# Two factorizations in one: the Gram matrix on the lower 64 partitions, the top block two steps behind on the upper 64

## The chip, the core and the metric

The kernel runs on one core of a Trainium2 chip. The core has TensorE (PE, matrix products), VectorE (DVE), ScalarE (ACT), GpSimd (POOL) and SyncE (SP, whose queue issues most of the transfers). The metric is the time of one execution in device microseconds (us). Less is better.

## The reference

An AdaLN transformer block over 16 batch items of 128 tokens with 144 channels, and then a rotation of its result in a subspace:

```python
x = _L0_cond_ref(x, cond[:, None, :], ...)   # layer norm, 16-head attention, MLP; shifts, scales, gates from cond
U, _ = jnp.linalg.qr(P)                      # P is 144 x 64
R = _rotation(cond, W, b)                    # expm of a skew 64 x 64 matrix, one for each item
z = jnp.einsum('btn,nd->btd', x, U)
z_rot = jnp.einsum('btd,bde->bte', z, R)
x_rot = x + jnp.einsum('btd,nd->btn', z_rot - z, U)
```

The change touches only `qr(P)`. The kernel takes U from an elimination of the Gram matrix G = P^T P (64 x 64). The signs that a Householder QR would give U's columns come from a second elimination, of the top 64 x 64 block B of P. B's elimination needs, at each step, the pivot of G's same step (its square root and the sign of B's own pivot give a shift of B's diagonal).

## The kernel before, in words

All instructions stand in an order written by hand, one stream for each engine, and semaphores connect them. An engine works through its stream in order: whatever stands behind a waiting instruction waits with it. After a front part (loads, modulations, weights transposed) comes a loop over b = 0 to 17, in which attention of item b, the rest of item b-1 and the output side of item b-2 are interleaved in four quarters q = 0 to 3. After it comes the MLP with the rotation. In the quarters of the loop stand also, one by one, the 64 steps of the elimination (`STEPS`: steps 0 to 2 stand in the front part, steps 3 to 63 in the quarters, with q = 3 left out at b = 4, 9 and 14), and from b = 0 on the stages of the matrix exponential.

The tile Z holds, on all 128 partitions, three blocks of 64 columns: G, an identity that becomes the inverse factor, and B. The matrices stand twice, on partitions 0 to 63 and again on 64 to 127. One step of the elimination does this:

- TensorE (`step_rows`) brings row k of G and row k-1 of B to all partitions: two products with a column of the identity repeated 128 times (lines 1440 and 1444), each an fp32 product that the trace shows as two MATMUL records.
- VectorE (`eliminations`) runs nine operations: G's step k and B's step k-1, interleaved, since B's step needs G's pivot of the step before. `s_Gstep` and `s_Bstep` tell that Z is updated.
- GpSimd computes in `square_root` the power -1/2 of the reciprocal pivot (line 412) and its double negated (413), and in `masked_column` B's column below the diagonal (417).

TensorE waits for the steps in `rows_read`, before each pair of step products. VectorE's quarters hold besides the step the maxima of the scores (`maximum`, line 969), layer norms and other work; the softmax maxima are what TensorE waits for next. The SyncE queue first issues the loads, then the store of the gates to memory and the load that spreads them over 128 partitions (`gates`, lines 331 and 334), then the 63 rows of the generator (`A<-v`, line 341), which VectorE reads in quarter 3 of b = 4 (`triangles`), and then waits for the outputs.

## Time and profile before

| | |
|---|---|
| median of 3 runs | 321.51 us (319.87 to 322.42) |
| span of the profiled execution | 323.8 us |
| TensorE busy | 282.6 us |
| VectorE busy | 212.7 us |
| ScalarE busy | 130.7 us |
| GpSimd busy | 105.0 us |
| mean granted clock of TensorE | 0.935 of full |

The span runs from the first to the last instruction of the profiled execution, which took 2.3 us more than the median run. A busy time is the time in which at least one of the engine's instructions ran. PEld is the loading of the stationary operand, which runs beside the products. The chain is the way back from the last instruction, at each step to what released it.

### The profile page before, as it was taken

How to read it: one execution, taken by the hardware profiler on the slowest of the kernel's cores; microseconds unless marked ns; L12 is line 12 of the kernel's file. 1: busy time of each engine (PE TensorE's matmuls, PEld its weight loads, DVE VectorE, ACT ScalarE, POOL GpSimd, SP SyncE). 2: the span in 40 equal slices, each digit the busy share in tenths (PEclk: the TensorE clock that was granted, in tenths of full speed). 3: DMA queues.
4: the chain of work that ended last, by engine and by line, in shares of the span. 5: the costliest groups of instructions: out<-in, count | busy, mean ns of one | idle time of the engine just before them, and what ended most of it. 6: DMA issues, size and time to landing. Idle time of an engine off the chain costs nothing.

```text
span 323.8 us, 8835 instructions
## 1 busy us (share of the span) xinstructions
PE 282.6 (87%) x3215; PEld 204.5 (63%) x3215; DVE 212.7 (66%) x948; ACT 130.7 (40%) x274; POOL 105.0 (32%) x298
## 2 busy tenths in 40 slices
PE   2898889879899998888998889989987489999995
PEld 2765355566666766647777567677775344756983
DVE  6147654785777998748997697757575665733543
ACT  1023323442555445416554444555444316340321
POOL 7413141524233324224442234323234088500000
PEclk9998967985999999959999999999999769999999
DMA  7936000000000000000000000000000000000013
GB/s 200 241 98 257 3 10 0 11 9 10 1 3 2 2 3 2 2 0 4 3 2 2 3 2 2 1 4 3 2 2 1 2 0 2 4 0 0 2 38 109
DMA packets 9779, 8.44 MB, mean 26 GB/s; under 512 B 2064, under 2 KB 9334, under 8 KB 9608
## 3 DMA queue, kind: packets, MB, share of 16 engines
q1 hardware_dynamic: 9380, 7.11, 7.7%
q10 hardware_dynamic: 356, 0.75, 0.8%
q8 instruction: 27, 0.44, 0.6%
q14 instruction: 16, 0.13, 0.1%
HBM read 6.40 MB, written 1.20 MB: 23 GB/s over the span
## 4 chain that ended last, share of the span: by engine, by line
PE 70%; DVE 20%; issue 6%; ACT 2%; POOL 1%; ACTq 1%; DVEq 0%
PE banks L1330 6%; PE banks L1440 6%; PE banks L1366 5%; PE banks L1598 5%; PE banks L1335 5%; PE banks L1331 5%; PE banks L1582 4%; PE banks L1198 4%; PE banks L1378 4%; PE banks L1444 3%; PE banks L1394 3%; DVE qstk L969 2%; DVE cB L914 2%; PE banks L1415 2%; PE banks L1404 2%
## 5 line engine op out<-in xcount | busy, mean ns | idle before, releaser
L412 POOL TENSOR_TENSOR root<-rec,mhalf 128x1 f32<-128x1 f32 x63 | 34.5, 548 | 151.0 <-DVE Z L910 151.0
L969 DVE TENSOR_REDUCE qstk<-banks 128x8 f32<-128x1024 f32 x32 | 39.0, 1219 | 7.9 <-PE banks L1366 6.3
L895 DVE RECIPROCAL rec<-banks 128x1 f32<-128x1 f32 x63 | 10.3, 164 | 46.0 <-PE banks L1444 43.0
L551 ACT ACTIVATE E<-banks 128x1024 f32<-128x1024 f32 x32 | 32.8, 1026 | 9.0 <-PE banks L1378 8.8
L1440 PE MATMUL banks<-Z,ident 128*128 128x65 f32 x126 | 26.6, 295 | 9.2 <-DVE Z L916 8.7
L1440 PEld LDWEIGHTS banks<-Z,ident 128*128 128x128 f32 x126 | 20.3, 201 | 18.5 <-issue 12.0
L1378 PEld LDWEIGHTS banks<-QM,KT 32*128 32x128 f32 x512 | 18.0, 193 | 16.5 <-issue 16.4
L1378 PE MATMUL banks<-QM,KT 32*128 32x128 f32 x512 | 24.2, 305 | 2.4 <-issue 2.4
L1366 PE MATMUL banks<-KT,QT 32*128 32x128 f32 x512 | 24.8, 310 | 1.7 <-DVE wskT L714 1.6
L1444 PE MATMUL banks<-Z,ident 128*128 128x64 f32 (+62 forms) x126 | 24.0, 272 | 0.4 <-DVE Z L916 0.4
L1366 PEld LDWEIGHTS banks<-KT,QT 32*128 32x128 f32 x512 | 18.4, 197 | 8.3 <-issue 8.3
L1394 PE MATMUL banks<-E,V 128*32 128x128 f32 x512 | 21.9, 292 | 1.4 <-ACT E L551 0.7
L1444 PEld LDWEIGHTS banks<-Z,ident 128*128 128x128 f32 x126 | 20.3, 202 | 0.6 <-issue 0.6
L1335 PE MATMUL banks<-ident,qstk 128*128 128x128 f32 x128 | 20.1, 282 | 0.0
L1330 PE MATMUL banks<-wqkv,hT 128*128 128x432 f32 x32 | 19.9, 709 | 0.0
L1598 PE MATMUL banks<-wfc2a,gT 128*128 128x144 f32 x128 | 18.6, 288 | 0.0
L1598 PEld LDWEIGHTS banks<-wfc2a,gT 128*128 128x128 f32 x128 | 16.7, 190 | 2.3 <-issue 2.3
L543 ACT ACTIVATE qstk<-banks 128x144 f32<-128x144 f32 x16 | 4.9, 309 | 32.2 <-PE banks L1331 32.2
L910 DVE SCALAR_TENSOR_TENSOR Z<-banks,cG,Z 128x64 f32<-128x64 f32 x63 | 17.8, 282 | 0.0
L509 ACT ACTIVATE hT<-banks,mod 128x128 f32<-128x128 f32 (+1 forms) x32 | 12.5, 445 | 12.9 <-PE banks L1317 12.9
L1331 PE MATMUL banks<-wqkv,hT 128*128 128x432 f32 x32 | 17.5, 633 | 0.0
L916 DVE SCALAR_TENSOR_TENSOR Z<-banks,cB,Z 128x63 f32<-128x63 f32 (+62 forms) x63 | 15.8, 251 | 2.2
(249 smaller groups left out, 627.2 us busy)
## 6 DMA issues: line engine op xcount, KB each, us to landing
gates<-gates_dram SPq DMA_DIRECT2D x1, 2304.0 KB, 9.7
x_all<-in_x_dram SPq DMA_DIRECT2D x4, 288.0 KB, 6.1
out_dram<-x_all SPq DMA_DIRECT2D x8, 144.0 KB, 2.0
wskew<-in_L_cond_W_dram SPq DMA_DIRECT2D x4, 283.5 KB
A<-v SPq DMA_DIRECT2D x63, 4.0 KB
wada<-in_L_cond_W_ada_dram ACTq DMA_DIRECT2D x1, 432.0 KB
wfc1a<-in_L_cond_W_fc_dram SPq DMA_DIRECT2D x1, 288.0 KB
wfc2a<-in_L_cond_W_fc_dram SPq DMA_DIRECT2D x1, 288.0 KB
```

The costliest lines, as they stand in the source:

```text
L412: link(nc.gpsimd.tensor_tensor(root[:, at], rec[:, at], mhalf[:, 0:1], ALU.pow))
L551: nc.scalar.activation(E[:, g, :, :, :].rearrange("p r j t -> p r (j t)"), scored(g), ACT.Exp).then_inc(s_E, 1)
L969: nc.vector.tensor_reduce(qstk[b % 2][:, 8 * g:8 * g + 8, D:D + 1].rearrange("p (j r) a -> p r (j a)", r=4), scored(g).rearrange("p r (j m ...
L1330: mm(bank[4][:, 0:3 * C], hT1[:, :], wqkv1[:, :], start=True, stop=False)
L1331: mm(bank[4][:, 0:3 * C], hT2[:, :], wqkv2[:, :], start=False, stop=True).then_inc(s_qkv, 1)
L1335: ins = pe.transpose(dst[:, 128 * j:128 * j + 128], stack[:, 4 * j:4 * j + 4, :].rearrange("p h s -> p (h s)"), ident[:, :])
L1366: ins = mm(bank[r][:, 128 * j:128 * j + 128], QT[rows, 2 * g + j, :], KT[b % 3][rows, 2 * g + j, :], start=True, stop=True)
L1378: ins = mm(bank[r][:, 128 * j:128 * j + 128], KT[b % 3][rows, 2 * g + j, :], QM[rows, 2 * g + j, :], start=True, stop=True)
L1394: ins = mm(bank[6][own, cols], weights[:, first:first + 32], E[:, g, 2 * (i % 2) + p, i // 2, :], start=(p == 0), stop=(p == 1))
L1440: mm(bank[7][:, cols], ident[:, k:k + 1].to_broadcast([128, 128]), Z[:, cols], start=True, stop=True).then_inc(s_Grow, 1)
L1444: mm(bank[7][:, cols], ident[:, k - 1:k].to_broadcast([128, 128]), Z[:, cols], start=True, stop=True).then_inc(s_Brow, 1)
L1598: mm(dst, gT[Q % 2][:, k, cols], wfc2a[:, k, :], start=(k == 0), stop=False)
```

## The change

G stays on partitions 0 to 63 and B moves to partitions 64 to 127, in the same columns but shifted by `SKEW` = 2: B's step k-2 is done in the same instructions as G's step k. So Z has 130 columns in place of 192, the steps are 65 in place of 64 (`LAST` = 64), and each has one chain of five VectorE operations over both halves. They are written in one form: a pivot is shifted by a signed amount, and for G that amount is zero, for B it is what G's step of two before gave. These four numbers for each of 64 rows travel in a DMA of 1 KB from `sent` (partitions 0 to 63) to `got` (partitions 64 to 127), with four buffers (`SHIFTS`). GpSimd now runs `elimination(k)`: the power, then `column_taken(k + 1)` (which waits for the transfer of step k-1), and two small operations that fill `sent`. The SyncE queue issues the 63 transfers, and the generator's 63 rows stand between them, seven at a time behind those of steps 11 to 19. The row products are 64x64 tiles. The skipped quarters are gone, and the last step stands at b = 15, q = 1. P and the Gram product are no longer doubled. At the end the two diagonals, now on different halves, are reduced into two columns and brought to all partitions by two small products.

The core of the diff:

```diff
     VS, VO = 48, 16
     SQ = 4
+    SKEW, SHIFTS = 2, 4
...
-        cB, c, w = sb("cB", [128, 1]), sb("c", [128, 1]), sb("w", [128, 1])
-        dG, dB, usc = sb("dG", [128, RD]), sb("dB", [128, RD]), sb("usc", [128, 4])
...
 
         v = sb("v", [B, NSK + 1])
         A0, Bm = sb("A0", [128, NC, RD]), sb("Bm", [128, NC, RD])
...
+                if FIRST + len(STEPS) <= LAST:
                     STEPS[b, q] = FIRST + len(STEPS)
-        assert FIRST + len(STEPS) == RD and max(STEPS) <= (B, 0)
+        assert FIRST + len(STEPS) == LAST + 1 and max(STEPS) <= (B, 0)
+
+        lower, upper_half, everywhere = slice(0, 64), slice(64, 128), slice(0, 128)
+
+        def half_of(k):
+
+            return lower if k < SKEW else everywhere if k < RD - 1 else upper_half
 
         def columns_left(k):
 
-            return slice(k + 1, RD + k + 1), slice(2 * RD + k, 3 * RD)
+            return slice(k + 1, RD + k + 1 if k < RD - 1 else RD + SKEW)
 
...
-            for i in range(RD - 1):
+            def generator_row(i):
                 at = (RD - 1) * i - i * (i - 1) // 2 - i
                 sp.wait_ge(s_v, min(4, (at + RD - 2) // 504 + 1))
                 sp.dma_start(A0[i:i + RD + 1:RD, :, :], v[:, at:at + RD]).then_inc(s_win, 16)
+
+            sp.wait_ge(k_fill, 8)
+            for j in range(RD - 1):
+                sp.wait_ge(s_sent, j + 1)
+                sp.dma_start(got[upper_half, j % SHIFTS, :], sent[:, j % SHIFTS, :]).then_inc(s_got, 16)
+                if ROWS_FROM <= j < ROWS_FROM + 9:
+                    for i in range(7 * (j - ROWS_FROM), 7 * (j - ROWS_FROM) + 7):
+                        generator_row(i)
 
...
+            def elimination(k):
+
+                own, at = sent[:, k % SHIFTS, :], slice(k, k + 1)
+                if k < RD - 1:
+                    pool.wait_ge(s_coef, k + 1)
+                    wait(pool, s_got, 16 * (k - SHIFTS + 1))
+                    rooted = lk.mark(nc.gpsimd.tensor_tensor(own[:, 2:3], rec[lower, at], mhalf[lower, 0:1], ALU.pow))
+                if k < LAST:
+                    pool.wait_ge(s_step, k + 1)
+                    column_taken(k + 1)
+                if k < RD - 1:
+                    lk.need(rooted)
+                    link(nc.gpsimd.tensor_tensor(own[:, 3:4], own[:, 2:3], coef[lower, at], ALU.mult))
+                    nc.gpsimd.tensor_tensor(own[:, 0:2], own[:, 2:4], own[:, 2:4], ALU.add).then_inc(s_sent, 1)
 
...
             def eliminations(k):
-                G, B = k < RD - 1, k > 0
-
-                if B:
-                    j, jp = bass.ds(k - 1, 1), bass.ds(k - 1 + 2 * RD, 1)
-                    bkk = bank[7][:, jp]
-                    dve.wait_ge(s_Brow, k)
-                if G:
-                    kk = bass.ds(k, 1)
-                    dve.wait_ge(s_Grow, k + 1)
-                    got_rec = lk.mark(nc.vector.reciprocal(rec[:, kk], bank[7][:, kk]))
-                if B:
-                    wait(dve, s_zm, k)
-                    got_c = lk.mark(STT(c[:, :], bkk, cG[:, j], zm[:, :], ALU.mult, ALU.subtract))
-                    wait(dve, s_root, k)
-                    got_sign = lk.mark(TS(cB[:, :], bkk, 0.0, nroot2[:, j], ALU.is_ge, ALU.mult))
-                if G:
-                    lk.need(got_rec)
-                    got_cG = lk.mark(TS(cG[:, kk], Z[:, kk], rec[:, kk], negmask[:, kk], ALU.mult, ALU.mult))
-                if B:
-                    lk.need(got_sign)
-                    got_pivot = lk.mark(STT(w[:, :], cB[:, :], root[:, j], bkk, ALU.add, ALU.subtract))
-                if G:
-                    lk.need(got_cG)
-                    cols = columns_left(k)[0]
-                    STT(Z[:, cols], bank[7][:, cols], cG[:, kk], Z[:, cols], ALU.mult, ALU.add).then_inc(s_Gstep, 1)
-                if B:
-                    lk.need(got_pivot)
-                    link(nc.vector.reciprocal(w[:, :], w[:, :]))
-                    link(STT(cB[:, :], c[:, :], w[:, :], cG[:, j], ALU.mult, ALU.add))
-                    cols = columns_left(k)[1]
-                    STT(Z[:, cols], bank[7][:, cols], cB[:, :], Z[:, cols], ALU.mult, ALU.add).then_inc(s_Bstep, 1)
+                own, at, cols = half_of(k), slice(k, k + 1), columns_left(k)
+                pivot = bank[7][own, at]
+                dve.wait_ge(s_row, k + 1)
+                dve.wait_ge(s_col, k + 1)
+                shift = got[own, (k - SKEW) % SHIFTS, :]
+                link(STT(signed[own, :], pivot.to_broadcast([own.stop - own.start, 2]), 0.0, shift[:, 0:2], ALU.is_ge, ALU.mult))
+                link(STT(den[own, :], pivot, signed[own, 0:1], shift[:, 2:3], ALU.add, ALU.subtract))
+                link(nc.vector.reciprocal(rec[own, at], den[own, :]))
+                TS(coef[own, at], signed[own, 1:2], rest[own, :], rec[own, at], ALU.add, ALU.mult).then_inc(s_coef, 1)
+                dve.wait_ge(s_coef, k + 1)
+                STT(Z[own, cols], bank[7][own, cols], coef[own, at], Z[own, cols], ALU.mult, ALU.add).then_inc(s_step, 1)
 
...
-                pe.wait_ge(s_ldP, 64)
-                mm(bank[7][:, 0:RD], twice(p1[:, :, :]), p1[:, 0, :], start=True, stop=False)
-                mm(bank[7][:, 0:RD], twice(p2[:, :, :]), p2[:, 0, :], start=False, stop=True)
-                mm(bank[7][:, RD:2 * RD], twice(p1[0:RD, :, :]), ident[0:RD, 0:RD], start=True, stop=True)
-                mm(bank[7][0:RD, 2 * RD:2 * RD + C1], p1[:, 0, :], ident[:, :], start=True, stop=True)
-                mm(bank[7][0:RD, 2 * RD + C1:2 * RD + C], p2[:, 0, :], ident[0:C2, 0:C2], start=True, stop=True).then_inc(s_Gp, 1)
+                pe.wait_ge(s_ldP, 32)
+                mm(bank[7][lower, 0:RD], p1[:, :], p1[:, :], start=True, stop=False)
+                mm(bank[7][lower, 0:RD], p2[:, :], p2[:, :], start=False, stop=True)
+                mm(bank[7][upper_half, 0:RD], p1[0:RD, :], ident[0:RD, 0:RD], start=True, stop=True)
+                mm(bank[7][0:RD, 2 * RD:2 * RD + C1], p1[:, :], ident[:, :], start=True, stop=True)
+                mm(bank[7][0:RD, 2 * RD + C1:2 * RD + C], p2[:, :], ident[0:C2, 0:C2], start=True, stop=True).then_inc(s_Gp, 1)
 
             pe.wait_ge(s_sil, 2)
             pe.transpose(bank[6][0:C1, 0:B], sil[:, 0:C1], ident[0:B, 0:B])
...
             def step_rows(k):
 
                 rows_read(k)
-                if k < RD - 1:
-                    cols = slice(k, RD + k + 1)
-                    mm(bank[7][:, cols], ident[:, k:k + 1].to_broadcast([128, 128]), Z[:, cols],
-                       start=True, stop=True).then_inc(s_Grow, 1)
-                if k > 0:
-                    cols = slice(2 * RD + k - 1, 3 * RD)
-                    mm(bank[7][:, cols], ident[:, k - 1:k].to_broadcast([128, 128]), Z[:, cols],
-                       start=True, stop=True).then_inc(s_Brow, 1)
+                own, cols = half_of(k), slice(k, columns_left(k).stop)
+                if own != upper_half:
+                    ins = mm(bank[7][lower, cols], ident[lower, k:k + 1].to_broadcast([RD, RD]), Z[lower, cols], start=True, stop=True)
+                if own != lower:
+                    at = RD + k - SKEW
+                    ins = mm(bank[7][upper_half, cols], ident[upper_half, at:at + 1].to_broadcast([RD, RD]), Z[upper_half, cols],
+                             start=True, stop=True)
+                ins.then_inc(s_row, 1)
 
...
             def U_parts(b, part):
                 if part == 0:
-                    pe.wait_ge(s_Bstep, RD - 1)
+                    pe.wait_ge(s_step, LAST + 1)
                     pe.wait_ge(s_QT, B)
                     pe.transpose(bank[4][0:RD, 512 - RD:512], Z[0:RD, RD:2 * RD], ident[0:RD, 0:RD]).then_inc(s_ETp, 1)
+                    pe.wait_ge(s_dred, 2)
+                    for own in (lower, upper_half):
+                        ins = mm(bank[4][own, 512 - RD - 2:512 - RD], eye2[:, :], dcol[:, :], start=True, stop=True)
+                    ins.then_inc(s_dgp, 1)
                 if part == 1:
                     pe.wait_ge(s_ET, 2)
+                    pe.wait_ge(s_dg, 1)
                     mm(bank[4][:, 0:C], twice(ET[:, :, :]), PT[:, :], start=True, stop=True).then_inc(s_UTp, 1)
                 if part == 2:
                     pe.wait_ge(s_UT, 2)
```

On TensorE, quarters 1 and 2 of block b = 5. A row names out and in by their tiles (Osb, kstk, qstk, KT, QT, E and V belong to the attention, A to the generator) and gives partitions and columns of the moving operand. Lines 1440 and 1444 are the step's row products. Before:

```order
L1404 MATMUL banks<-ident,Osb 128x128 x2
L1440 MATMUL banks<-Z,ident 128x65
L1444 MATMUL banks<-Z,ident 128x42
L1335 MATMUL banks<-ident,kstk 128x128 x4
L1335 MATMUL banks<-ident,qstk 128x128 x4
L1366 MATMUL banks<-KT,QT 128x128 x8
L1394 MATMUL banks<-E,V 32x128 x8
L1204 MATMUL banks<-eye,A 64x64 x16
L1440 MATMUL banks<-Z,ident 128x65
L1444 MATMUL banks<-Z,ident 128x41
```

After, the same place:

```order
L1412 MATMUL banks<-ident,Osb 128x128 x2
L1447 MATMUL banks<-Z,ident 64x65
L1450 MATMUL banks<-Z,ident 64x65
L1343 MATMUL banks<-ident,kstk 128x128 x4
L1343 MATMUL banks<-ident,qstk 128x128 x4
L1374 MATMUL banks<-KT,QT 128x128 x8
L1402 MATMUL banks<-E,V 32x128 x8
L1212 MATMUL banks<-eye,A 64x64 x16
L1447 MATMUL banks<-Z,ident 64x65
L1450 MATMUL banks<-Z,ident 64x65
```

The pair of step products keeps its place. Each of the two is now a 64-partition tile with 65 columns at every step, where the second of the pair had 42 and 41 columns here.

On VectorE, the first step of block b = 0 and what stands around it: `wskT` is the last copy of the front part, `qstk` the first maximum. Before:

```order
L714 COPY wskT<-banks 16x504
L969 TENSOR_REDUCE qstk<-banks 128x4x2
L895 RECIPROCAL rec<-banks 128x1
L898 SCALAR_TENSOR_TENSOR c<-banks,cG,zm 128x1
L900 TENSOR_SCALAR cB<-banks,nroot 128x1
L903 TENSOR_SCALAR cG<-Z,rec,negmask 128x1
L906 SCALAR_TENSOR_TENSOR w<-cB,root,banks 128x1
L910 SCALAR_TENSOR_TENSOR Z<-banks,cG,Z 128x64
L913 RECIPROCAL w<-w 128x1
L914 SCALAR_TENSOR_TENSOR cB<-c,w,cG 128x1
L916 SCALAR_TENSOR_TENSOR Z<-banks,cB,Z 128x61
```

After:

```order
L739 COPY wskT<-banks 16x504
L977 TENSOR_REDUCE qstk<-banks 128x4x2
L916 SCALAR_TENSOR_TENSOR signed<-banks,got 128x2
L917 SCALAR_TENSOR_TENSOR den<-banks,signed,got 128x1
L918 RECIPROCAL rec<-den 128x1
L919 TENSOR_SCALAR coef<-signed,rest,rec 128x1
L921 SCALAR_TENSOR_TENSOR Z<-banks,coef,Z 128x64
```

The step's nine rows are five, and each waits for the one before it; the place of the step behind the maximum is the same.

On the SyncE queue, from the store of the gates on. Before:

```order
L331 DMA gates_dram<-gates_sb 16x288
L334 DMA gates<-gates_dram 128x4608
L341 DMA A<-v 2x8x64 x63
L346 DMA out_dram<-x_all 128x2x144 x8
L93 UNCONDITIONAL_BRANCH
```

After (the pattern of seven generator rows and one `got` goes on nine times, and the rest of the `got` rows follow):

```order
L336 DMA gates_dram<-gates_sb 16x288
L339 DMA gates<-gates_dram 128x4608
L350 DMA got<-sent 64x4 x12
L345 DMA A<-v 2x8x64 x7
L350 DMA got<-sent 64x4
L345 DMA A<-v 2x8x64 x7
L350 DMA got<-sent 64x4
L345 DMA A<-v 2x8x64 x7
```

The transfers of the steps stand behind the load of the gates, and the generator's rows stand between them.

## Rows read from the trace of the kernel before

**Rows 1.** The page: busy times, TensorE clock, and the chain that ended last.

```profile
PE 282.6 (87%) x3215; PEld 204.5 (63%) x3215; DVE 212.7 (66%) x948; ACT 130.7 (40%) x274; POOL 105.0 (32%) x298
...
PEclk9998967985999999959999999999999769999999
...
PE 70%; DVE 20%; issue 6%; ACT 2%; POOL 1%; ACTq 1%; DVEq 0%
PE banks L1330 6%; PE banks L1440 6%; PE banks L1366 5%; PE banks L1598 5%; PE banks L1335 5%; PE banks L1331 5%; PE banks L1582 4%; PE banks L1198 4%; PE banks L1378 4%; PE banks L1444 3%; PE banks L1394 3%; DVE qstk L969 2%; DVE cB L914 2%; PE banks L1415 2%; PE banks L1404 2%
```

**Rows 2.** The chain in order of time, 110 to 170 us: start us, us, what.

```profile
116.69 0.17 PE banks L1440 x2
116.86 0.21 PE banks L1444 x2
...
120.87 0.17 DVE rec L895
...
121.88 0.23 DVE cB L914
...
122.14 0.27 DVE Z L916
122.40 0.14 issue
122.54 0.41 PE banks L1440 x2
122.94 0.20 PE banks L1444 x2
...
132.12 1.08 PE banks L1198 x32
133.20 0.37 PE banks L1440 x2
```

**Rows 3.** The page, costliest groups: line engine out<-in count | busy, mean ns | idle before.

```profile
L412 POOL TENSOR_TENSOR root<-rec,mhalf 128x1 f32<-128x1 f32 x63 | 34.5, 548 | 151.0 <-DVE Z L910 151.0
```

**Rows 4.** DMA issues: what, queue, count, KB each, median us to landing.

```profile
gates<-gates_dram SPq DMA_DIRECT2D x1, 2304.0 KB, 9.7
x_all<-in_x_dram SPq DMA_DIRECT2D x4, 288.0 KB, 6.1
...
p<-in_L_cond_P_dram SPq DMA_DIRECT2D x2, 4.0 KB, 4.3
...
gates_dram<-gates_sb SPq DMA_DIRECT2D x1, 18.0 KB, 1.4
cond_sb<-in_cond_dram SPq DMA_DIRECT2D x1, 9.0 KB, 2.1
```

**Rows 5.** Timeline, VectorE, 26 to 28.5 us: end of step 2, last weight copy.

```profile
27.34 0.28 DVE L916 SCALAR_TENSOR_TENSOR Z<-banks,cB,Z 128x62 f32<-128x62 f32 x1
27.54 0.66 DVE L714 COPY wskT<-banks 16x504 f32<-16x504 f32 x1
```

**Rows 6.** Timeline, TensorE: the first scores.

```profile
28.34 0.73 PE L1366 MATMUL banks<-KT,QT 32*128 32x128 f32 x16 [1.57 <-DVE wskT L714]
```

**Rows 7.** Timeline, SyncE queue: the load of the gates, the first generator rows.

```profile
22.91 0.34 SPq L334 DMA_DIRECT2D gates<-gates_dram  x1
37.60 4.45 SPq L341 DMA_DIRECT2D A<-v  x8
```

**Rows 8.** Windows of 2 us: busy times and counts, PEclk, DMA share, GB/s.

```profile
26.00:28.00 2.00, 0.77 (x8) 0.45 (x5) 1.93 (x11) 1.19 (x3) 0.87 (x3) 1.00 0.87 304
...
30.00:32.00 2.00, 2.00 (x4) 0.76 (x4) 1.74 (x10) 0.00 (x0) 0.67 (x2) 0.50 0.15 65
```

**Rows 9.** Timeline, VectorE: the first instruction of step 11.

```profile
62.82 0.16 DVE L895 RECIPROCAL rec<-banks 128x1 f32<-128x1 f32 x1
```

**Rows 10.** Timeline, TensorE: the row product in quarter 0 of block 5.

```profile
100.52 0.43 PE L1440 MATMUL banks<-Z,ident 128*128 128x65 f32 x2
```

**Rows 11.** Timeline, VectorE, quarter 0 of block 16: the inverse factor copied.

```profile
246.48 0.35 DVE L948 COPY ET<-banks 64x64 f32<-64x64 f32 x2 [1.70 <-PE banks L1469]
```

More of the change, by code:

```diff
@@ L382, in _ @@
                 diagonal(eye2[own, :], own)
-            for own in (lo, hi):
-                below_diagonal(negmask[own, :], own, -1.0)
+            for own, base in ((lo, 0), (hi, -SKEW)):
+                below_diagonal(below[own, :], own, -1.0, base)
             for own in (lo, hi):
@@ L456, in attention @@
                         scales_of_U()
+            pool.wait_ge(s_Z, 4)
+            column_taken(0)
             for k in range(FIRST):
-                square_root(k)
-                masked_column(k)
+                elimination(k)
             for b in range(0, B + 2):
```

90 lines of the change are left out of this document (44 added, 46 removed).

## The prediction

> **What bounds the kernel now.** I began with the page. TensorE is busy for 87% of the span, and the chain that ended last is 70% TensorE and 20% VectorE [rows 1]. So the reader should see a kernel in which one in-order engine sets most of the time and another holds it up at places. The elimination is in both shares. Its row products (L1440 and L1444) are 6% and 3% of the chain, some 29 us, and one operation of the VectorE step (L914) alone is 2%, some 6.5 us, which at 0.23 us each [rows 2] is 28 steps. Counted piece by piece, the chain goes through 51 pairs of row products and about 25 VectorE steps. Split by time (28 to 61, 61 to 100, 100 to 246 us) they are 7, 9 and 35 pairs, and 4, 6 and 15 steps. What the change does to these is its gain. GpSimd and the SyncE queue are nearly absent from the chain, and the change puts both into the loop of the steps. That is where its cost must be looked for.
>
> **Row products.** On the chain a pair costs 0.38 us where the work ahead has the same tile shape (0.17 + 0.21) and 0.61 us when it follows a wait (0.41 + 0.20); the mean over the 35 late pairs is 0.52 [rows 2]. The new pair is four records of 64x64 tiles. Such tiles stand in the trace: 32 of L1198 take 1.08 us, 0.034 each, and the 128x128 product behind them takes 0.37 in place of 0.17, so a change of tile shape costs 0.2 us [rows 2]. The new pair is then 0.14 us, plus some 0.06 on the way in and 0.15 to 0.2 on the way out: 0.34 on the mean, a gain of 0.18. Between the score products and the values it gains more; in quarter 1, which had no change of shape before, it gains nothing. Bounds: if the two halves don't overlap, 0.47 (gain 0.05); if the way out is hidden, 0.2 (gain 0.3).
>
> **VectorE step.** From the first operation to the end of Z the nine operations take 122.41 - 120.87 = 1.54 us, two chains interleaved. The five new ones wait for one another. A dependent operation costs 0.26 us from start to start (121.88 to 122.14) [rows 2], a reciprocal less, so I take four times 0.24 plus 0.27: 1.23 us, a gain of 0.3. Bounds: five ninths of 1.54 (gain 0.7) and no gain.
>
> **GpSimd's column.** VectorE's next step now waits also for `column_taken`, which stands behind the power (0.55 us [rows 3]) on GpSimd. The power starts with `coef`, some 0.3 us before Z is done, so the column is ready about 0.55 us after Z. TensorE's way from the end of Z to the next step is 0.14 + 0.61 us before [rows 2] and about 0.5 after. The two are level, and I charge nothing; if GpSimd is 0.2 us later, the waited steps cost 0.2 x 25 = 5 us.
>
> **The transfer.** It is issued after the column of step k+1 is taken, and the column of step k+2 waits for it. So a column can follow the last after 0.65 us on GpSimd plus the transfer L. The smallest transfers in the trace took 1.4 us (18 KB, the queue empty) and 2.1 us (9 KB read from memory) [rows 4]; I take L = 1.8, nearer to neither. The loop is then 2.45 us (2.05 to 2.75). The steps of quarters 1 and 3 in a late block stand 122.54 - 116.69 = 5.85 us apart, 2.9 us for one [rows 2], and after the change 2.8 with the gains above. So in these blocks the transfer costs nothing at L = 1.8, and nothing up to L = 2.15. The Trainium skill (DMA: Bandwidth & Descriptors, section "Anatomy of one DMA — SWDGE (gpsimd) path") gives a fixed cost of about 2.0 us for one DMA. With that as L the loop would be 2.65 us, still under 2.8, and only the landing in the paragraph on the generator's rows would move, by 0.2 us, which makes the forecast 322.2; no transfer of this size stands in the trace of before to decide it.
>
> **The start.** The first transfer is needed by step 2, which stands on VectorE ahead of the last weight copy, and TensorE's first scores wait for that copy [rows 5, 6]. On SyncE it stands behind the load of the gates, issued at 22.9 us [rows 7] and landed 9.7 us later [rows 4], at 32.6. That a small transfer waits for a large one on its queue shows in P's 4 KB, which took 4.3 us behind the 288 KB of x_all, against 1.4 on an empty queue [rows 4]. I let the transfer land at 32.0 (31.0 to 32.9: most of the gates' bytes have moved by 31 [rows 8]). Then come column 0.3, step 1.2, copy 0.66 and the semaphore 0.14: scores at 34.3 in place of 28.34, **+6.0 us** (0 if it isn't held).
>
> **The generator's rows.** Eight take SyncE 4.45 us, 0.55 each [rows 7]. Seven and one transfer (0.45) are 4.3 us, and this goes on nine times, while the twelve quarters from step 11 to block 5 take 100.5 - 62.8 = 37.7 us, 3.1 each [rows 9, 10]. Step 11 starts at 62.8, so its transfer goes out at 65.1 (step 1.54, GpSimd 0.75), and that of step 20 at 65.1 + 9 x 4.3 = 103.8. It lands at 105.6; step 22 starts at 105.9 and ends at 107.1; TensorE's next row product, in quarter 0 of block 5, starts at 107.3 in place of 100.52, **+6.8 us**. The queue is behind from the second transfer on, so what the steps gain between 61 and 100 us (9 x 0.18 + 6 x 0.3 = 3.4) is lost in it and not counted. Bounds: +6 to +8, by L.
>
> **Small terms.** Three of the Gram products load half the columns: -0.7 us, hidden by nothing. Steps now stand in the quarters 3 of blocks 9 and 14 (+1.0) and none in quarters 2 and 3 of block 15, where the chain went through the last two steps (-1.6). At the end TensorE and VectorE wait for the diagonals (two products, a copy; a like pair of copies is 0.35 [rows 11]): +1.0.
>
> **The clock.** TensorE idled from 26.8 to 28.3 us [rows 6], and soon after, the granted clock was 0.5 of full, 1.2 GHz in place of 2.4 [rows 8]. The page's clock line has several such dips [rows 1]. The 7 us of idling at the start and the waits in blocks 3 and 4 should lengthen them: +1.5 us (0 to 7).
>
> **The sum.** Gains outside blocks 2 to 4: pairs 42 x 0.18 = 7.6, steps 19 x 0.3 = 5.7: -13.3. Against them +6.0 + 6.8 + 1.0 + 1.5, and -0.7 - 0.6: 323.8 + 0.7 = 324.5 us of span. The profiled execution was 2.3 us above the median, so the forecast is **322 us**: what the steps gain is spent on the SyncE queue.
>
> **Rivals.**
> - Not held: the first transfer passes the gates' load, since its 64 short pieces share the engines with it. The 4.3 us of P speak against that. It gives 322.2 - 6.0 = 316 us.
> - Bigger gain: VectorE's step near 1.0 us and the way out hidden. 42 x 0.1 + 19 x 0.2 = 8 more, 314 us. For it speaks that 28 steps lie on the chain; against it the four dependencies.
> - **Transfer-bound (slower):** on the GpSimd-SyncE loop, with L = 2.4 us the loop takes 3.05 us, 0.25 more than a late step would have. Over the 42 steps behind the generator's rows that is +10.5 us: 332 us. It decides from L = 2.15 on. The 2.1 us of a small load [rows 4] are close to that; the 1.4 us of the store speak against it.
> - Clock: the new idling keeps TensorE at 1.2 GHz through half of blocks 3 to 5. The dips on the page's clock line to 5 and 6 in ten [rows 1] show that it can stay down for whole slices of 8 us. +5: 327 us.
> - The halves don't overlap, so that the pair does not do what it is made for: 42 x 0.13 = +5.5, 328 us.
>
> **How the numbers follow.** A measurement of this kernel can tell about 1%, 3.2 us, from no change. Forecast 0.37 (318.5 to 324.7); not held 0.14; bigger gain 0.13; transfer-bound 0.12; clock 0.18; no overlap 0.06. Faster by over 1%: 0.27. Within: 0.37. Slower: 0.36. With cases of both signs the forecast's own range stands beside the full one: 313 takes in both faster cases; 330 takes in the clock and the overlap case and leaves out most of the transfer-bound one and the tails of the others, under 2 in 10.
>
> **What would show it.** The first `got` should land after 31 us, with TensorE idle from 27 to 34. In blocks 2 to 4 the `got` issues should be 4.3 us apart, and GpSimd's column should be what VectorE waits for. Later blocks should be 0.8 to 1 us shorter than the 12.2 of before, with `column_taken` waiting for no transfer; the four records of a pair should start within 0.15 us. I am wrong if the start has no hole, if the generator rows are issued faster between transfers, or if late steps wait for `got`.

## The result and the profile after

The changed kernel takes **334.1 us** (median of 4 runs, 331.0 to 335.6) against 320.7 us (318.9 to 322.4) for the kernel before: a ratio of 1.040, 95% interval 1.032 to 1.049. It is slower, and above the forecast's range. Some executions of each kernel run up to 3% longer at a lower granted clock; the ranges here hold all runs, the ratios leave those out. The experiments were run later, in four groups, each beside the kernel before. Its medians there are 323 to 325 us with a wider spread (319 to 330), but its fastest run is 319.0 to 320.1 in every group, and 318.9 above. The changed kernel was not run again, so an experiment's distance from its 334.1 is a distance between groups.

The page of the changed kernel, in the parts that answer to [rows 1, 3, 4] (on top its span, then busy times, clock, chain, costliest groups, DMA issues):

```profile
span 332.7 us, 8806 instructions
...
PE 270.1 (81%) x3219; PEld 184.6 (55%) x3219; DVE 192.9 (58%) x709; ACT 130.5 (39%) x274; POOL 125.8 (38%) x363
...
PEclk9998599999779589799999997999979769999999
...
PE 40%; issue 14%; DMA 12%; SPq 11%; POOL 11%; DVE 9%; ACT 1%; ACTq 1%; POOLq 0%; DVEq 0%
DMA got<-sent 11%; SPq L345 9%; PE banks L1610 5%; POOL rest L425 4%; PE banks L1594 4%; PE banks L1374 3%; PE banks L1206 2%; PE banks L1338 2%; POOL sent L434 2%; PE banks L1386 2%; PE banks L1339 2%; PE banks L1343 2%; PE banks L1402 2%; PE banks L1447 1%; POOL sent L441 1%
...
L916 DVE SCALAR_TENSOR_TENSOR signed<-banks,got 128x2 f32<-128x2 f32 (+1 forms) x65 | 10.1, 156 | 67.8 <-POOL rest L425 41.1
L425 POOL TENSOR_SCALAR rest<-Z,below,got 128x1 f32<-128x1 f32 (+1 forms) x65 | 26.0, 400 | 49.2 <-DMA got<-sent 47.4
...
L1374 PE MATMUL banks<-KT,QT 32*128 32x128 f32 x512 | 25.5, 317 | 9.2 <-DVE wskT L739 9.1
L1447 PE MATMUL banks<-Z,ident 64*64 64x65 f32 x126 | 20.6, 245 | 13.3 <-DVE Z L921 12.8
...
gates<-gates_dram SPq DMA_DIRECT2D x1, 2304.0 KB, 9.8
...
got<-sent SPq DMA_DIRECT2D x63, 1.0 KB, 1.6
A<-v SPq DMA_DIRECT2D x63, 4.0 KB
```

Read it from the chain. TensorE's share falls from 70% to 40%, and VectorE's from 20% to 9%. In their place stand the transfer (`got`, 11%), the SyncE queue's row issues (L345, 9%) and GpSimd (11%). The work itself did become cheaper (TensorE is busy for 12.5 us less, VectorE for 20), but the chain left it. The groups name the waits in their order: GpSimd's column waited 47.4 us for transfers, VectorE's step 41.1 us for the column, TensorE 12.8 us for the step. Between 62 and 126 us the chain is nearly half (49.3%) row issues of line 345.

The start, in the timelines of the SyncE queue, GpSimd, VectorE and TensorE (start us, us, what, idle before and its releaser):

```profile
23.09 0.34 SPq L339 DMA_DIRECT2D gates<-gates_dram  x1
23.54 11.02 SPq L350 DMA_DIRECT2D got<-sent  x2
...
33.26 0.39 POOL L425 TENSOR_SCALAR rest<-Z,below,got 128x1 f32<-128x1 f32 x1 [8.08 <-DMA got<-sent]
...
33.76 0.16 DVE L916 SCALAR_TENSOR_TENSOR signed<-banks,got 128x2 f32<-128x2 f32 x1 [7.68 <-POOL rest L425]
...
34.72 0.28 DVE L921 SCALAR_TENSOR_TENSOR Z<-banks,coef,Z 128x64 f32<-128x64 f32 x1
34.92 0.66 DVE L739 COPY wskT<-banks 16x504 f32<-16x504 f32 x1
...
35.72 1.24 PE L1374 MATMUL banks<-KT,QT 32*128 32x128 f32 x16 [9.08 <-DVE wskT L739]
```

The first transfer, 1 KB, is issued 0.45 us behind the load of the gates and lands 9.6 us later. TensorE's first scores are at 35.72 in place of 28.34 [rows 6], and take 1.24 us in place of 0.73, since TensorE was granted 1.2 GHz (0.50) from 36 to 38 us.

The generator's rows, in the timelines of the SyncE queue, VectorE and TensorE, from 90 us:

```profile
90.06 0.53 SPq L350 DMA_DIRECT2D got<-sent  x1
90.63 3.76 SPq L345 DMA_DIRECT2D A<-v  x7
94.44 0.53 SPq L350 DMA_DIRECT2D got<-sent  x1
...
107.53 0.53 SPq L350 DMA_DIRECT2D got<-sent  x1
...
93.44 0.16 DVE L916 SCALAR_TENSOR_TENSOR signed<-banks,got 128x2 f32<-128x2 f32 x1 [4.36 <-POOL rest L425]
...
94.73 0.27 PE L1447 MATMUL banks<-Z,ident 64*64 64x65 f32 x1 [3.44 <-DVE Z L921]
```

From 90 us on a transfer leaves every 4.37 us, and one step of the elimination follows each. Windows of the changed kernel by stage, from the first scores of block 0, 3, 4, 5, 6 and 15 to the next (columns as in [rows 8]), and under them those of the kernel before for the same stages:

```profile
35.72:74.40 38.68, 33.04 (x335) 18.55 (x335) 24.59 (x93) 15.36 (x33) 16.85 (x52) 0.94 0.02 3
74.40:90.56 16.16, 11.46 (x139) 7.55 (x138) 8.46 (x33) 5.98 (x14) 6.42 (x19) 0.89 0.04 8
90.56:108.47 17.91, 11.60 (x140) 7.51 (x139) 7.81 (x27) 6.00 (x14) 5.48 (x18) 0.90 0.05 9
108.47:126.08 17.61, 14.03 (x172) 9.31 (x171) 9.75 (x34) 5.99 (x14) 6.18 (x21) 0.71 0.02 2
126.08:240.62 114.54, 103.01 (x1632) 74.39 (x1631) 81.15 (x275) 59.06 (x126) 53.86 (x166) 0.97 0.02 3
240.62:332.70 92.08, 77.90 (x702) 54.05 (x701) 47.24 (x161) 30.89 (x62) 23.86 (x50) 0.93 0.05 14
```

```profile
28.34:75.12 46.78, 41.20 (x335) 26.65 (x335) 31.04 (x153) 15.71 (x33) 13.61 (x43) 0.80 0.06 22
75.12:89.33 14.21, 12.93 (x139) 9.29 (x139) 8.59 (x42) 5.79 (x14) 4.39 (x14) 0.81 0.02 5
89.33:99.87 10.54, 10.02 (x136) 7.30 (x135) 8.60 (x38) 6.09 (x14) 4.14 (x15) 1.00 0.01 3
99.87:112.14 12.27, 11.51 (x171) 8.81 (x170) 9.50 (x43) 5.91 (x14) 3.53 (x12) 1.00 0.01 1
112.14:232.71 120.57, 109.53 (x1623) 83.41 (x1623) 91.41 (x404) 59.26 (x127) 42.13 (x128) 0.97 0.01 2
232.71:323.80 91.09, 77.80 (x707) 54.35 (x707) 49.66 (x180) 30.75 (x62) 24.72 (x54) 0.94 0.05 14
```

The 8.9 us between the two spans are +7.4 at the start, -8.1 in blocks 0 to 2, +14.7 in blocks 3 to 5, -6.0 in blocks 6 to 14, and +1.0 behind. Much of the -8.1 is the clock (0.80 there before, 0.94 after). Experiment 10 is the kernel before with its late steps left out, the same up to block 8. Its blocks 0 to 2 take 41.1 us and its blocks 3 to 5 35.2 (here 46.8 and 37.0). Against that trace the change is -2.4 and +16.5. Of the -6.0, 4.1 us lie in block 8 (15.3 before, 11.2 after), where the granted clock was 0.79 before and 1.00 after.

The medians lie 4.5 us further apart than the spans. In the runs that have both, the time is some 1.8 us more than the span. The profiled execution before, by its span of 323.8, was then one of some 325.6 us, 4.9 above its median, by those low clocks; the one after took 334.5, 0.4 above. (The 2.3 us that were counted between the profiled and the median run set a span against a time. Time against time they are 4.1, and the forecast stays what it is, since its own span of 324.5 is a time of 326.3.)

### The profile page after: what moved, and what is told of

The parts are those of the page before. It is cut to its first block, busy times and chain, and to the rows that moved or that the text cites. A ratio compares the mean times of both kernels' runs of the same rounds, so it can differ in the third digit from the quotient of the medians.

```text
span 332.7 us, 8806 instructions
## 1 busy us (share of the span) xinstructions
PE 270.1 (81%) x3219; PEld 184.6 (55%) x3219; DVE 192.9 (58%) x709; ACT 130.5 (39%) x274; POOL 125.8 (38%) x363
## 4 chain that ended last, share of the span: by engine, by line
PE 40%; issue 14%; DMA 12%; SPq 11%; POOL 11%; DVE 9%; ACT 1%; ACTq 1%; POOLq 0%; DVEq 0%
DMA got<-sent 11%; SPq L345 9%; PE banks L1610 5%; POOL rest L425 4%; PE banks L1594 4%; PE banks L1374 3%; PE banks L1206 2%; PE banks L1338 2%; POOL sent L434 2%; PE banks L1386 2%; PE banks L1339 2%; PE banks L1343 2%; PE banks L1402 2%; PE banks L1447 1%; POOL sent L441 1%
## 5 line engine op out<-in xcount | busy, mean ns | idle before, releaser
L434 POOL TENSOR_TENSOR sent<-rec,mhalf 64x1 f32<-64x1 f32 x63 | 34.6, 550 | 85.4 <-DVE coef L919 85.4
L916 DVE SCALAR_TENSOR_TENSOR signed<-banks,got 128x2 f32<-128x2 f32 (+1 forms) x65 | 10.1, 156 | 67.8 <-POOL rest L425 41.1
L425 POOL TENSOR_SCALAR rest<-Z,below,got 128x1 f32<-128x1 f32 (+1 forms) x65 | 26.0, 400 | 49.2 <-DMA got<-sent 47.4
L1447 PE MATMUL banks<-Z,ident 64*64 64x65 f32 x126 | 20.6, 245 | 13.3 <-DVE Z L921 12.8
L1447 PEld LDWEIGHTS banks<-Z,ident 64*64 64x64 f32 x126 | 12.4, 137 | 26.0 <-issue 13.3
L1450 PE MATMUL banks<-Z,ident 64*64 64x65 f32 (+2 forms) x126 | 20.6, 244 | 0.0
L921 DVE SCALAR_TENSOR_TENSOR Z<-banks,coef,Z 128x64 f32<-128x64 f32 (+2 forms) x65 | 18.3, 282 | 2.3
L1338 PE MATMUL banks<-wqkv,hT 128*128 128x432 f32 x32 | 19.1, 685 | 0.0
L919 DVE TENSOR_SCALAR coef<-signed,rest,rec 128x1 f32<-128x1 f32 (+1 forms) x65 | 17.7, 273 | 2.4
L1343 PEld LDWEIGHTS banks<-ident,qstk 128*128 128x128 f32 x128 | 15.4, 145 | 6.4 <-issue 6.2
L533 ACT ACTIVATE hT<-banks,mod 128x128 f32<-128x128 f32 (+1 forms) x32 | 12.5, 444 | 11.9 <-PE banks L1325 11.9
```

Source lines behind the costliest of these rows:

```text
L425: nc.gpsimd.tensor_scalar(rest[own, :], Z[own, at], below[own, at], got[own, (k - SKEW) % SHIFTS, 3:4], ALU.mult, ALU.subtract).then_inc(s ...
L434: rooted = lk.mark(nc.gpsimd.tensor_tensor(own[:, 2:3], rec[lower, at], mhalf[lower, 0:1], ALU.pow))
L1338: mm(bank[4][:, 0:3 * C], hT1[:, :], wqkv1[:, :], start=True, stop=False)
L1343: ins = pe.transpose(dst[:, 128 * j:128 * j + 128], stack[:, 4 * j:4 * j + 4, :].rearrange("p h s -> p (h s)"), ident[:, :])
L1447: ins = mm(bank[7][lower, cols], ident[lower, k:k + 1].to_broadcast([RD, RD]), Z[lower, cols], start=True, stop=True)
```

## The experiments

Theory A is the forecast's own: what is late is the SyncE queue, where the transfers stand behind the gates' load and then behind seven rows each. Rivals: the DMA engines are full whatever the queue (B), the clock and the operations queued behind GpSimd's waiting column (C, L), and the transfer's latency in every step (D). The edits are of the changed kernel unless said. The starts of each block's first scores, in us, are read from one execution each; those of 3, 4 and 11 are the longest of their runs (324.4, 323.0 and 309.8 us):

| kernel | median | b0 | b3 | b5 | b6 | b9 | b15 | span |
|---|---|---|---|---|---|---|---|---|
| before | 320.7 | 28.3 | 75.1 | 99.9 | 112.1 | 154.4 | 232.7 | 323.8 |
| changed | 334.1 | 35.7 | 74.4 | 108.5 | 126.1 | 163.2 | 240.6 | 332.7 |
| 1 gates, ScalarE's queue | 330.8 | 28.2 | 71.7 | 105.6 | 121.6 | 157.3 | 234.6 | 326.4 |
| 2 gates, pieces | 323.4 | 27.8 | 66.2 | 100.7 | 113.9 | 149.6 | 227.0 | 320.6 |
| 3 rows spread | 321.2 | 35.9 | 74.8 | 99.0 | 116.2 | 153.3 | 230.4 | 322.6 |
| 4 skew four | 319.0 | 27.9 | 66.0 | 91.4 | 112.5 | 149.6 | 226.3 | 321.2 |
| 5 = 2 + 3 | 313.6 | 28.2 | 66.8 | 92.2 | 104.2 | 139.9 | 217.6 | 311.2 |
| 6 = 2 + 3 + 4 | 311.5 | 30.3 | 66.3 | 87.4 | 104.6 | 140.3 | 215.6 | 309.9 |
| 7 zeroing first | 331.5 | 34.1 | 74.3 | 108.7 | 123.8 | 159.3 | 237.1 | 330.6 |
| 11 = 6 + later masking | 306.5 | 30.0 | 66.6 | 88.6 | 100.1 | 137.2 | 214.0 | 308.0 |
| 12 = 5 + later masking | 310.6 | 27.7 | 67.3 | 92.1 | 104.2 | 139.9 | 215.8 | 308.0 |

### 1. The gates' load on ScalarE's queue

```diff
-            sp.dma_start(gates[:, :, :].rearrange("p b n -> p (b n)"),
-                         gd.to_broadcast([128, B * 2 * C])).then_inc(s_gld, 16)
...
                 generator_weights(n)
+                if n == 0:
+                    act.wait_ge(s_gst, 16)
...
+                    act.dma_start(gates[:, :, :].rearrange("p b n -> p (b n)"),
+                                  gd.to_broadcast([128, B * 2 * C])).then_inc(s_gld, 16)
```

> Only edit: the 2304 KB load of gates is issued by ScalarE's queue (behind its first copy of the generator's weights) instead of SyncE's, so that the small transfers of got no longer stand behind it in a queue. Theory A (the order of one queue made the start late): the first transfer lands about 2 us after its issue at 23.5, the first scores start near 28.5 to 29.5 instead of 35.7, and the run is 5 to 7 us below the changed kernel's 334.1: 327 to 329. Rival B (the load fills the 16 DMA engines, whichever queue it is in): the first transfer still takes 7 us or more, first scores after 33, 331 to 334.

Measured: 330.8 us (328.2 to 335.6). ScalarE's queue, GpSimd and TensorE in its timelines:

```profile
23.38 0.35 ACTq L622 DMA_DIRECT2D gates<-gates_dram  x1
...
33.54 0.37 POOL L421 TENSOR_SCALAR rest<-Z,below,got 128x1 f32<-128x1 f32 x1 [5.71 <-DMA got<-sent]
...
28.24 0.73 PE L1375 MATMUL banks<-KT,QT 32*128 32x128 f32 x16 [1.31 <-DVE wskT L740]
...
35.32 0.37 PE L1448 MATMUL banks<-Z,ident 64*64 64x65 f32 x1 [4.45 <-DVE Z L922]
```

The transfer issued ahead of the load passes (1.65 us), and the scores are at 28.24. The next one, issued at 26.3 us, takes 7.1 us with no load ahead of it on its queue, and the hole comes back one step later: block 0 takes 17.9 us in place of 13.3. So A named the wrong thing. B was right in that the wait is for the load itself, and another queue only moves it; its late first scores (after 33) did not come, since here the first transfer goes out ahead of the load. The Trainium skill (DMA: Bandwidth & Descriptors, section "Queues, rings and completion order") says that each DMA engine serves the queues in turns, a whole packet of descriptors at a time. If an engine's share of this load were one packet or little more, that would account for the 7.1 us; no run here shows the packets' bounds.

### 2. The gates' load in sixteen pieces

```diff
-            sp.dma_start(gates[:, :, :].rearrange("p b n -> p (b n)"),
-                         gd.to_broadcast([128, B * 2 * C])).then_inc(s_gld, 16)
+
+            def gates_piece(b):
+                sp.dma_start(gates[:, b, :], gates_dram[b:b + 1, :].to_broadcast([128, 2 * C])).then_inc(s_gld, 16)
...
                 sp.dma_start(got[upper_half, j % SHIFTS, :], sent[:, j % SHIFTS, :]).then_inc(s_got, 16)
+                if j < B // 2:
+                    gates_piece(2 * j)
+                    gates_piece(2 * j + 1)
```

> Only edit: the load of gates is cut into 16 loads of 144 KB, two behind each of the first eight transfers of got on SyncE's queue. Each transfer then stands behind at most two loads (about 1.2 us together, a 16th of 9.8 us each). Theory A (one queue's order) and rival B (the DMA engines are full) both expect the first scores near 29 to 31 and 327 to 330 for the run; if it stays above 332, the start isn't what costs and the gain of an earlier start is given back in blocks 3 to 6.

Measured: 323.4 us (322.2 to 325.9), 10.7 below the changed kernel, and below the 327 to 330 that both theories expected. No transfer takes over 2.8 us up to 60 us, and the scores are at 27.8. Block 0 takes 11.4 us at the full 2.4 GHz (13.3 at 0.83 in the changed kernel). This belongs to the hole: wherever the start is late by it (the changed kernel, 3, 7, 8) block 0 takes 13.2 to 13.4 us at 0.79 to 0.83, and wherever the load is in pieces (2, 5, 6, 11, 12) 11.3 to 11.4 at 1.00. So the hole costs 7.9 + 1.9 us, more than its own length. The trace has 4.0 us less in blocks 3 to 5 too, all in block 5 (13.2 for 17.6), and 1.5 more in blocks 1 and 2. Those 4.0 us can't be put down to the hole, since experiment 8 has the hole and a block 5 of 12.5 us (rows in the next section).

### 3. The generator's rows, four behind each of 16 transfers

```diff
-        ROWS_FROM = FIRST + 8
+        ROWS_FROM = FIRST + 3
-                if ROWS_FROM <= j < ROWS_FROM + 9:
-                    for i in range(7 * (j - ROWS_FROM), 7 * (j - ROWS_FROM) + 7):
+                if ROWS_FROM <= j < ROWS_FROM + 16:
+                    for i in range(4 * (j - ROWS_FROM), min(4 * (j - ROWS_FROM) + 4, RD - 1)):
```

> Only edit: the 63 generator rows are issued 4 behind each of 16 transfers (steps 6 to 21) instead of 7 behind each of 9 (steps 11 to 19). SyncE's cycle in that stretch is then 0.5 + 4 x 0.54 = 2.7 us instead of 4.37. Theory A (SyncE's issues set the pace of blocks 2 to 5): the steps no longer come 4.37 us apart, block 6 starts 8 to 13 us earlier than the changed kernel's 126.1 relative to block 2, and the run gives 321 to 326. Rival C (the stage is late through the throttled clock and through what is queued behind the waiting column on GpSimd, whatever the rows' number): 330 to 334.

Measured: 321.2 us (319.6 to 324.4), 13.0 below. Blocks 3 and 4 take 12.5 and 11.7 us in place of 16.2 and 17.9. Theory A holds, and C does not: neither the start's hole nor the operations behind the column were touched. Nor is the length of these blocks a matter of the clock. In the five traces with seven rows behind each of nine transfers at a skew of two (the changed kernel, 1, 2, 7, 8) blocks 3 and 4 together take 33.9 to 34.6 us, at granted clocks from 0.69 to 0.90. Blocks 3, 4 and 5 of experiment 8, which is the changed kernel up to block 8:

```profile
76.63:91.75 15.12, 12.04 (x140) 8.13 (x139) 7.64 (x29) 5.99 (x14) 6.09 (x17) 0.77 0.04 7
91.75:110.83 19.08, 14.15 (x139) 9.61 (x138) 7.91 (x27) 5.98 (x14) 5.78 (x19) 0.73 0.05 8
110.83:123.36 12.53, 10.91 (x171) 7.66 (x171) 9.76 (x34) 5.99 (x14) 5.93 (x21) 1.00 0.02 3
```

In experiment 3 block 5 stays long (17.1 us, 0.80 of the clock); VectorE waits 2.3 us for the last rows there, of which experiments 6 and 11 show more.

### 4. A skew of four steps

```diff
-    SKEW, SHIFTS = 2, 4
+    SKEW, SHIFTS = 4, 8
```

with one semaphore for each of four transfers in flight, and without GpSimd's wait for an old transfer ahead of the power.

> Only edit: the upper half runs four steps behind instead of two (eight slots for the carried values, one semaphore for each of four transfers in flight, two steps more at the end), so that a column waits for a transfer three steps old. Gates load and generator rows stay as they are. Theory D (in the late blocks the transfer's latency in the loop GpSimd, SyncE, DMA, GpSimd eats the gain): blocks 7 to 15 shorten by 0.5 to 0.8 us each, 5 to 8 us, and the start gains 2 to 5 us as steps 1 to 3 wait for no transfer; in all 320 to 328. Rival E (late blocks are bound by other work, the wait for the transfer has cover): blocks 7 to 15 shorten by less than 0.2 us each, and only the start gains: 329 to 333.

Measured: 319.0 us (316.4 to 323.0), 15.1 below, below what either theory expected. The gates' load still holds the first transfer for 9.6 us, but no step up to 3 needs it, and the hole is gone. Blocks 8 to 14 keep their lengths (11.2, 11.5, 14.5, 12.7, 13.3, 12.5, 12.2 us against 11.2, 11.6, 14.6, 12.7, 13.3, 12.5, 12.7). The sum that E made, 329 to 333, was wrong by blocks 3 and 4, which a deeper skew also shortens (25.4 us for 34.1); block 5 is longer (21.0 for 17.6), with a wait of 5.1 us for the last rows. But D falls and E holds for what they were to tell apart: in the late blocks the transfer's latency is covered at a skew of two, though GpSimd waits for it there (14.8 us in 21 waits behind 126 us, in the changed kernel).

### 5 and 6. Both repairs, at a skew of two and of four

> Both repairs of SyncE's queue together, at the change's own skew of two steps: gates in 16 pieces behind the first eight transfers, and the generator rows 4 behind each of 16 transfers. The loads of gates end with step 7, the rows begin at step 6, so in two steps both stand behind a transfer. Each repair alone gave 323.4 and 321.2 against the changed kernel's 334.1. Theory F (the two delays are separate, 7.5 us at the start and 9 to 13 us in blocks 3 to 5, and the rest is the granted clock): together 310 to 316. Rival G (what one saves, the other loses: TensorE's clock or the steps' chain takes a part back, as the load on ScalarE's queue did, where the start gained 7.5 and block 0 lost 4.6): 317 to 322.

> Both repairs and a skew of four steps (the sum of the three edits). If a transfer is still waited for in blocks 0 to 5 at a skew of two, with 4 rows behind each, this lies 2 to 4 us under the kernel with both repairs at skew two; if the two steps' slack already covers it, the two are the same within 1 us. In blocks 8 to 15 the length of a block should not change, as it didn't with the skew alone (11.2, 11.5, 14.5, 12.7, 13.3, 12.5, 12.2 against 11.2, 11.6, 14.6, 12.7, 13.3, 12.5, 12.7).

Measured: 313.6 us (313.0 to 314.3) at a skew of two, 0.979 of the kernel before (0.971 to 0.987); 311.5 at four (three runs of 311.2 to 312.1 and one of 305.8), at the near edge of the 2 to 4 us that it was to gain if the transfers were still waited for. Theory F holds: the two delays nearly add up (10.7 + 13.0 = 23.7 apart, 20.6 together). At a skew of four block 5 takes 17.2 us. VectorE and TensorE in that trace:

```profile
91.41 0.69 DVE L752 TENSOR_TENSOR A<-A,upper 128x512 f32<-128x512 f32 x1 [3.55 <-DMA A<-v]
...
93.34 1.23 PE L1390 MATMUL banks<-QM,KT 32*128 32x128 f32 x16 [2.75 <-issue]
```

VectorE is held by the first reader of the rows, `triangles`, until the last of them lands. What stood in the transfers' way is now itself late: its 63 issues of some 0.5 us, with the transfers between them, run from 45 to 90 us.

### 7. The zeroing of qstk ahead of the column

```diff
+                    if q == 0 and within(b, 1, B - 2):
+                        column_cleared(b - 1)
                     if (b, q) in STEPS:
                         elimination(STEPS[b, q])
...
-                    if q == 0 and within(b, 1, B - 2):
-                        column_cleared(b - 1)
```

> The changed kernel, with one edit on GpSimd: in quarter 0 of each block the zeroing of qstk's column comes ahead of the elimination's part instead of behind it, so that it is no longer queued behind a column that waits for a transfer. TensorE waited 4.6 us in all for this zeroing, 2.3 and 0.9 us of it in blocks 3 and 4. Theory A: in blocks 2 to 5 SyncE's issues set the pace, so that this wait only takes up time that the next step would have waited anyway: 332 to 335, no change. Rival L (what stands behind the waiting column makes the stage late): 328 to 331, blocks 3 and 4 shorter by 2 us or more.

Measured: 331.5 us (328.4 to 332.5), 1.025 of the kernel before (1.017 to 1.034). TensorE's 3.2 us of waiting for `qstk` between 60 and 130 us are gone, but 4.1 us of waiting ahead of row products, released by VectorE's `ON`, have come, and blocks 3 and 4 are as long as they were (16.5 and 17.9 us). The median lies between the two ranges expected, and the 2.6 us are inside the spread of the runs. L, which asked for 2 us from these blocks, fails.

### 8 to 10. What the steps cost in blocks 9 to 14

Both kernels without the elimination's steps from block 9 on; this leaves out part of the factorization.

> The changed kernel with no elimination steps from block 9 on (work left out: the factorization stops at step 38, so that the output isn't the reference's), all else as it is. It says what the steps cost in blocks 9 to 14. Theory H (the steps have nearly no price left there, because other chains set the blocks' length): these six blocks, 77.4 us in the changed kernel, take 73 to 76, that is at most the four pairs of row products of 0.26 us, 1.0 us per block, less where TensorE waits for an evacuation anyway. Rival I (the steps' chain through VectorE and GpSimd is still on the path): 70 or less.

> The kernel before with no elimination steps from block 9 on (work left out in the same way; the output isn't the reference's). Its six blocks 9 to 14 take 78.3 us. Theory H: they come down to the same 73 to 76 us as the changed kernel without steps, and the difference of the two falls (78.3 less this, 77.4 less that) is all that the cheaper steps could give there: about 1 us of the 6 that a sum by single operations gave. Rival I: they fall to 70 or less.

> The kernel before with no elimination steps from block 9 on, once more (work left out, the output isn't the reference's), since the trace of the first attempt came from an execution of 596.6 us in which every TensorE instruction took more than twice its time. Without its steps the changed kernel's blocks 9 to 14 took 69.0 us instead of 77.4: 8.4 us, 0.35 per step. The kernel before has 22 steps there and 78.3 us. If its steps cost as much as their pairs of row products (0.55 us each), the six blocks take 66 to 67 us; if they fall to the same 69.0 us as the changed kernel without steps (the more likely, as all that is left is the same work), its steps cost 9.2 us, 0.42 each, and the change's step is only 0.07 us cheaper on the path in these blocks, not the 0.48 of the forecast.

Changed kernel without these steps: 323.7 us (322.6 to 327.2). Kernel before without them: the first attempt gave 319.3 us and, in the execution that was profiled, 596.6, so that no stage can be read from it; the second 310.6 us (310.3 to 311.0). Why 319.3 lies 9 us above that, no trace shows. The sums over blocks 9 to 14 (the last line of the windows' view), changed without steps, before without steps, changed and before with them:

```profile
sum 69.04, PE 61.51 PEld 45.49 DVE 29.86 ACT 39.24 POOL 6.25; mean PE 10.25 PEld 7.58 DVE 4.98 ACT 6.54 POOL 1.04
```

```profile
sum 68.69, PE 61.50 PEld 45.50 DVE 29.61 ACT 39.23 POOL 6.31; mean PE 10.25 PEld 7.58 DVE 4.94 ACT 6.54 POOL 1.05
```

```profile
sum 77.42, PE 69.60 PEld 50.49 DVE 53.06 ACT 39.79 POOL 35.08; mean PE 11.60 PEld 8.41 DVE 8.84 ACT 6.63 POOL 5.85
```

```profile
sum 78.27, PE 71.94 PEld 55.71 DVE 58.53 ACT 39.94 POOL 26.72; mean PE 11.99 PEld 9.29 DVE 9.75 ACT 6.66 POOL 4.45
```

The floors agree within 0.4 us. Above them 22 steps cost 9.6 us before (0.44 each) and 24 cost 8.4 after (0.35), or 6.9 (0.29) in experiment 12, where all six blocks ran at a clock of 1.00, as in the kernel before (0.92 to 1.00 in the changed kernel). Theory H, 73 to 76 us, was wrong: the steps did have a price of their own, and rival I was right. The saving is 0.09 a step here, 0.15 at equal clock. In blocks 6 and 7 it is 0.3: 27.0 us before, 24.5 in experiment 12, both at 0.98 of the clock or more.

### 11 and 12. The later masking, at a skew of four and of two

```diff
-                    if q == 3 and b == MATRIX - 1:
+                    if q == 0 and b == MATRIX:
                         triangles()
```

> The kernel with both repairs and a skew of four, and one more edit: VectorE's masking of the generator (the first reader of the 63 rows) moves from quarter 3 of block 4 to quarter 0 of block 5, behind the maximum and the step. In the kernel without this edit VectorE waited 3.6 us at 87.9 for the last rows, which landed at 91.4, TensorE stood 2.7 us and then ran at 0.5 of its clock until 100: block 5 took 17.2 us. Theory J (SyncE's 63 row issues of 0.54 us fill its time from 45 to 90 and are now late for their reader; nothing else binds block 5): block 5 takes 11.5 to 13 us and the run lies 4 to 5 us lower: 305 to 308 against the 311.5 measured. Rival K (the clock falls in block 5 anyway): the wait goes, but block 5 stays at 15 us or more, 309 to 312.

> Both repairs of SyncE's queue and the later masking of the generator, at the change's own skew of two steps; beside the kernel with a skew of four (306.5 us) it says what the skew is still worth once SyncE's queue is clear. The transfer's loop at a skew of two was 2.63 us in the changed kernel, a block at full clock has 10.5 to 11.5 us for four steps, 2.6 to 2.9 each, and up to four rows of 0.54 us can stand ahead of a transfer in blocks 1 to 4. If this cover is enough: 306 to 308. If it is not, blocks 2 to 4 are 1 us longer each, as in the kernel with the two repairs alone (13.4, 11.1, 14.3 us against 12.4, 11.5, 10.5): 309 to 312.

Measured: **306.5 us** (304.7 to 309.8) at a skew of four, 0.951 of the kernel before (0.944 to 0.957); 310.6 (309.1 to 317.0) at two, 0.971 (0.954 to 0.988). Only experiment 11 has its whole interval below 0.98. The median of 306.5 alone would prove little, as one run of experiment 6 took 305.8; the traces show more. Block 5 takes 11.5 us at a clock of 1.00 (17.2 at 0.80 in experiment 6), so J holds: its long time came from the wait for the rows and the low clock behind it. At a skew of two blocks 4 and 5 take 23.4 us (26.3 in experiment 5). There blocks 2 and 3 are 14.4 and 13.5 us against 12.4 and 11.5 at a skew of four, at lower clocks (0.87 and 0.76 against 0.95 and 0.90): where rows stand between transfers, the deeper skew is still worth 4 us. Experiment 11 beats both kernels.

## Why the prediction was wrong

The sum, term by term, against the two profiled spans (blocks 6 to 14: 35 x 0.18 + 15 x 0.3 - 1.0; behind: 1.6 - 1.0):

| stage | forecast | measured |
|---|---|---|
| start | +6.0 | +7.4 |
| blocks 0 to 2 | -2.5 | -8.1 |
| blocks 3 to 5 | +6.8 | +14.7 |
| blocks 6 to 14 | -9.8 | -6.0 |
| behind | -0.6 | +1.0 |
| Gram, clock | +0.8 | in the others |
| sum | +0.7 | +8.9 |

Against the trace of experiment 10, blocks 0 to 2 are at -2.4, as forecast, and blocks 3 to 5 at +16.5.

- **What was right.** The mechanism: the gains are spent on the SyncE queue. VectorE's step takes 35.00 - 33.76 = 1.24 us (1.23 forecast). The rows' cycle is 4.37 us (4.3), and the halves' records start within 0.15 us. The transfer is harmless in late blocks, by experiment 4, though not for the reason given: GpSimd does wait for it, which was named as a sign of being wrong, and the wait has cover.
- **The start** was sized well as a hole. What its end costs was not: TensorE comes out of it at 1.2 GHz, and block 0 is 1.9 us longer by it. 10.7 us measured by experiment 2, 6.0 forecast and 1.5 for the clock everywhere.
- **The step that failed: "The generator's rows", +6.8.** The term was mis-sized. It runs from step 11 on VectorE (64.80 us; 62.82 before) to the row product in quarter 0 of block 5 (112.35). That is 47.5 us, where the forecast had 44.5 and the kernel before 37.7: +9.8, not +6.8 (46.4 to 49.2 us in the other four traces with these rows at this skew). The cycle was nearly right. Too short were the way to the first transfer (2.9 us, not 2.3), the nine cycles (39.8, not 38.7), the last transfer's landing (2.9, not 1.8) and the way from there to step 22 (0.65, not 0.3). And it ended the loss at that row product, where the trace shows TensorE standing from 110 to 112 us and granted 1.2 GHz until 118. The rest of block 5 takes 13.7 us; in experiment 8, with the same instructions at a clock of 1.00, 11.0. Experiment 3 gives 13.0 us for this stage, where the term and the 3.4 us of gains that it counted as lost make 10.2.
- **The clock**, +1.5 (0 to 7), was charged as one small term: 1.9 us in block 0 and up to 2.7 in block 5, inside its range. The mean granted clock hardly fell (0.935 before, 0.928 after), and in blocks 3 and 4 a lower clock costs nothing, since the queue sets their length. So the rival "Clock" was not what made the kernel slow.
- **The queue and the gains together.** From the changed kernel to experiment 12 are 23.5 us, to experiment 11 27.6. For the two queue terms, the clock and the 3.4 us lost with them the forecast had 17.7; without them it would have been 304.3, where experiment 12, at the change's own skew, gave 310.6, and experiment 11 306.5. So 6 to 10 of the 12 us that the forecast missed are the queue's and its holes', and the rest is gains that were too large. The pair of row products gained more than its 0.18: behind the scores it was 0.55 us and is 0.26. But in blocks 9 to 14 the price of a whole step fell by 0.09 to 0.15 us only, where the terms make it some 0.3. That TensorE there waits for other operations in the time that a cheaper step frees is the likely reason; no run shows it.
- **Transfer-bound**, the rival above 330, gave 332 us, near the result, by luck: the transfer took 1.6 us, not 2.4, and the loop 2.63 (rest to rest, 33.26 to 35.89). The 2.0 us fixed cost of the Trainium skill (DMA: Bandwidth & Descriptors, section "Anatomy of one DMA — SWDGE (gpsimd) path"), which the page gives for transfers issued by GpSimd, is above the 1.6 measured for these, issued by SyncE. Less the transfer that loop has 1.0 us, where the forecast had 0.65; the column alone takes 0.36 of it.
- What stays open: what the low clock alone costs. Experiment 8 against the changed kernel gives 2.7 us for the rest of block 5, but no run changes the clock and nothing else, and none shows why the clock was back in one execution and not in the other.

## What to carry to other kernels

A small transfer put into a serial loop takes the place that its queue and the DMA engines give it: list everything that is issued or moved in its whole lifetime, not only around the step, and either cut that into pieces between the transfers or leave the loop more slack; here this made 1.04 of the old time into 0.95. Follow a delay to the end of the stretch where the clock is back, and price a hole of TensorE with that stretch. One trace of each kernel is not enough to price a stage: compare the same blocks in every run whose code is the same there. When the first user of a queue is relieved, look who is last on it then (here the masking that waited for the rows).
